# A language-model tower on one core: the front stage's VectorE and ScalarE queues in another order

## The reference

```python
h = L0_tok_W_with_zero_row[x]                        # out-of-range tokens give a row of zeros
# RWKV block on xn = layernorm(h)
xx = shift_by_one_token(xn)
k = (xn*mix_k + xx*(1-mix_k)) @ Wk.T                 # v and r alike
def step((p, q, o), (kt, vt)):
    no = max(o, u + kt)
    y  = (exp(o-no)*p + exp(u+kt-no)*vt) / (exp(o-no)*q + exp(u+kt-no))
    no2 = max(w + o, kt)                             # the running maximum
    return (exp(w+o-no2)*p + exp(kt-no2)*vt, exp(w+o-no2)*q + exp(kt-no2), no2), y
h = h + (sigmoid(r) * y) @ Wo.T
# the next block, on x1 = layernorm(h)
logits = x1 @ w_router.T                             # 4 experts
probs = softmax(logits); gate, idx = top_k(probs over the tokens, 256 of 512)
y = layernorm(x1) * gamma1 + beta1                   # then attention, MLP and the scatter back
```

## Time and profile before

| | |
|---|---|
| median of 3 runs | 2375.97 us |
| the profiled execution: its own time, its span | 2375.98 us, 2374.2 us |
| TensorE busy | 2081.6 us, 88% |
| VectorE busy | 1209.1 us, 51% |
| ScalarE busy | 775.0 us, 33% |
| GpSimd busy | 514.9 us, 22% |
| 100 to 200 us: TensorE, VectorE busy, granted clock | 88.03, 70.64 us, 0.81 |
| 200 to 300 us: the same | 57.61, 76.41 us, 0.59 |
| 300 to 400 us: the same | 31.39, 70.11 us, 0.57 |

### The profile page before, as it was taken

The page is one execution under the profiler, slowest core; times in us unless marked ns, Lnnn a source line. Parts: engine busy times, 40 slices in busy tenths (PEclk is TensorE's granted clock), DMA queues, the critical chain, the costliest instruction groups (busy, mean ns, idle before and its releaser), DMA issues. The chain is left out here.

```text
span 2374.2 us, 29716 instructions
## 1 busy us (share of the span) xinstructions
PE 2081.6 (88%) x10840; PEld 1304.1 (55%) x10848; DVE 1209.1 (51%) x2811; ACT 775.0 (33%) x1330; POOL 514.9 (22%) x718
## 2 busy tenths in 40 slices
PE   4887516899898899986999999879999999999997
PEld 2343313354454454444566666546555878787885
DVE  5776866655755765634766776535711222222221
ACT  2212101445445444544455555312111111111111
POOL 5100113231331322101111111110072222222222
PEclk9977556999999999997999999978999999999999
DMA  3600000000000000000000000020023122222221
GB/s 65 226 11 0 0 1 12 1 1 1 1 1 1 1 1 1 1 1 25 5 6 6 5 6 5 5 90 1 7 87 100 29 60 61 58 55 55 66 33 18
DMA packets 42131, 66.10 MB, mean 28 GB/s; under 512 B 10362, under 2 KB 34206, under 8 KB 39713
## 3 DMA queue, kind: packets, MB, share of 16 engines
q1 hardware_dynamic: 25858, 48.43, 6.3%
q0 software_dynamic: 16128, 15.76, 3.9%
HBM read 35.66 MB, written 30.03 MB: 28 GB/s over the span
## 5 line engine op out<-in xcount | busy, mean ns | idle before, releaser
L1288 ACT ACTIVATE e<-c_ps_s 128x512 f32<-128x512 f32 x384 | 220.6, 598 | 254.0 <-PE c_ps_s L1114 253.2
L928 DVE TENSOR_REDUCE row_max<-c_ps_m 128x1 f32<-128x512 f32 x384 | 255.4, 686 | 63.4 <-PE c_ps_m L1098 57.4
L2585 DVE TENSOR_TENSOR e_f<-e_ps_u,e_gate 128x512 f32<-128x512 f32 x120 | 83.0, 692 | 309.4 <-ACT e_gate L2828 309.4
L2828 ACT ACTIVATE e_gate<-e_ps_g 128x512 f32<-128x512 f32 x120 | 71.6, 597 | 441.2 <-PE e_ps_g L2755 441.2
L2386 POOL DMA_INDIRECT out<-m_o,m_row_of x80 | 125.6, 1570 | 304.8 <-issue 282.8
L1098 PE MATMUL c_ps_m<-c_kT,qT 96*128 96x512 bf16 x384 | 153.5, 400 | 27.2 <-DVE row_max L928 26.2
L1114 PE MATMUL c_ps_s<-qT,c_kT 97*128 97x512 bf16 x384 | 150.1, 393 | 25.5 <-DMA qT<-max_rows 15.1
L2769 PE MATMUL e_ps_o<-m_w,e_f 128*128 128x192 f32 x960 | 166.7, 331 | 1.4 <-DVE e_f L2585 1.4
L2769 PEld LDWEIGHTS e_ps_o<-m_w,e_f 128*128 128x128 f32 x960 | 154.9, 190 | 14.7 <-issue 12.9
L2759 PE MATMUL e_ps_u<-m_xT,m_w 64*128 64x256 f32 x480 | 135.3, 402 | 0.0
L2755 PE MATMUL e_ps_g<-m_xT,m_w 64*128 64x256 f32 x480 | 135.3, 402 | 0.0
(11 more groups left out here) (427 smaller groups left out, 4065.9 us busy)
## 6 DMA issues: line engine op xcount, KB each, us to landing
dealt<-x SPq DMA_DIRECT2D x8, 1290.0 KB, 13.4
m_x<-dealt SPq DMA_DIRECT2D x40, 258.0 KB, 2.7
m_w<-in_w13e SPq DMA_DIRECT2D x8, 1152.0 KB, 5.4
m_w<-in_w2e SPq DMA_DIRECT2D x8, 576.0 KB, 6.6
out<-h SPq DMA_DIRECT2D x8, 384.0 KB, 4.6
c_twice<-conv SPq DMA_DIRECT2D x16, 128.0 KB, 2.3
out<-m_o,m_row_of POOLq DMA_INDIRECT x80, 3.5
e_s<-in_s SPq DMA_DIRECT2D x1, 1152.0 KB, 6.2
```

The lines of the kernel that those rows point to most:

```text
L928: dve.tensor_reduce(row_max[:, n // J, n % J:n % J + 1], ps_m[:, n % 2, :], AX_X, ALU.max)\
L1288: act.activation(e[:, n % LIVE_E, :], ps_s[:, n % 2, :], ACT.Exp, scale=QSCALE).then_inc(e_ready, 1)
```

## The change

On VectorE, exponents 0 moves ahead of the loop, and in the loop exponents p+1 stands behind norm_sums p-1 and ahead of add_rows p. For the last pair, in the same place, stand the statistics and the application of the second block's layernorm (`moe.y`), which were at the end. On ScalarE, the copies of keys p+1 stay together, and exps p+1 stands behind gates p+1 and ahead of routed p-1. On GpSimd, the reciprocal root for `moe.y` moves ahead of the last two of the layernorms in `roots`. TensorE's and SyncE's queues, all sizes and all arithmetic stay.

```diff
--- before.py
+++ after.py
@@ -316,10 +316,11 @@
             kit.apart(pool)
             gather(2)
             gather(3)
-            for n in range(4, 4 * PAIRSEQ, 2):
+            for n in range(4, 4 * PAIRSEQ - 2, 2):
                 roots(n)
             pool.wait_ge(y_var, 1)
             ln_rstd(kit, pool, moe.rstd, moe.var_eps).then_inc(y_rstd, 1)
+            roots(4 * PAIRSEQ - 2)
             pool.wait_ge(moe_in, 7 * 16)
             pool.wait_ge(y_norm, 1)
             y = moe.y[:, :, 0:C]
@@ -453,8 +454,8 @@
 
             norm_rows(0)
             norm_rows(1)
+            exponents(0)
             for p in range(PAIRSEQ):
-                exponents(p)
                 if p + 2 < PAIRSEQ:
                     norm_rows(p + 2)
                 if p > 1:
@@ -462,13 +463,16 @@
                 weighted_means(p)
                 if p > 0:
                     norm_sums(p - 1)
+                if p + 1 < PAIRSEQ:
+                    exponents(p + 1)
+                else:
+                    ln_stats(dve, x1[:, 0:J, :], moe.stats, moe.mv, moe.var_eps, 1e-6).then_inc(y_var, 1)
+                    dve.wait_ge(y_rstd, 1)
+                    ln_apply(dve, moe.y[:, :, 0:C], x1[:, 0:J, :], moe.mv, moe.rstd).then_inc(y_norm, 1)
                 add_rows(p)
             norm_sums(PAIRSEQ - 1)
-            ln_stats(dve, x1[:, 0:J, :], moe.stats, moe.mv, moe.var_eps, 1e-6).then_inc(y_var, 1)
             read_logits(PAIRSEQ - 2)
             dve.memset(ones, 1.0)
-            dve.wait_ge(y_rstd, 1)
-            ln_apply(dve, moe.y[:, :, 0:C], x1[:, 0:J, :], moe.mv, moe.rstd).then_inc(y_norm, 1)
             read_logits(PAIRSEQ - 1)
 
             dve.drain()
@@ -681,18 +685,14 @@
             gates(0)
             for p in range(PAIRSEQ):
                 if p + 1 < PAIRSEQ:
-                    keys(p + 1, 0)
-                    keys(p + 1, 1)
-                    if p > 0:
-                        exps(p)
-                    keys(p + 1, 2)
+                    for i in range(3):
+                        keys(p + 1, i)
                     if p + 2 < PAIRSEQ:
                         turned(p + 2)
                     for i in range(3):
                         values(p + 1, i)
                     gates(p + 1)
-                else:
-                    exps(p)
+                    exps(p + 1)
                 if p > 0:
                     routed(p - 1)
             routed(PAIRSEQ - 1)
```

## The result

| | before | changed | ratio, 95% interval |
|---|---|---|---|
| median of 4 and 4 runs | 2377.18 us | 2360.14 us (2355.1 to 2366.1) | 0.9928 [0.9902, 0.9954] |
| same kernels, second series (11 and 6 runs) | 2380.16 us | 2362.55 us (2351.5 to 2367.3) | 0.9908 [0.9884, 0.9932] |
| same kernels, third series (11 and 6 runs) | 2378.55 us | 2360.20 us (2353.1 to 2366.7) | 0.9918 [0.9900, 0.9935] |

What follows compares the result with a forecast made beforehand. VectorE was taken to carry the front stage's chain, idle 31.7 us for output matmuls and 16.0 us for ScalarE's exponentials. Gains of 7.4, then 23.7, shrinking to 22.3 us in all gave 2375.98 - 22.3 = 2353.7 us, range 2349.5 to 2358.5.

Steps and rivals of the forecast that it cites:

- Pair 0 to 1: Exponents 1 fill VectorE's wait for outputs 0, so `num` of pair 1 starts at 112.9 instead of 120.33 us.
- term of 7.4 us: Gain at the weighted means of pair 1: the 7.5 us of idle time ahead of the additions, less a gap.
- Pair 1 to 2: `num` of pair 2 at 165.2 instead of 188.86 us, 23.7 us gained in all, despite 7.0 us new wait for logits.
- Rival 2: Pair 0's logits find the clock low and take 8.3 instead of 6.0 us: 2356.0 us; chance 0.11.
- Pair 2 to 3: `num` of pair 3 at 219.7 instead of 241.97 us; TensorE idles some 5 us before logits, gain shrinks to 22.3 us.
- The tail: From z of pair 3 to the last read, TensorE carries the chain; the moved `moe.y` work costs nothing there.
- The starting point: The sum started from the profiled execution's 2375.98 us; the median was 2375.97 us.
- The range: 2349.5 to 2358.5 us, from the clock in two groups of logits and the gaps; leaves out two rivals.
- my nine: The forecast's range for the program's time, 2349.5 to 2358.5 us.
- Rival 1: Pair 1's logits find the clock high and take 6.0 us: 2351.4 us; chance 0.16.
- rival 3: TensorE becomes the bound in pair 3, k, v, r staying at half clock: 5.9 us slower, 2381.9 us; chance 0.04.
- rival 4: The gain is given back behind the stage, by the clock or transfers meeting otherwise: 2376 us; chance 0.05.

Runs made afterwards that it cites:

- profile 1: The changed kernel without further edit, first series: last read of logits at 292.90 us, ratio to before 0.9928 [0.9902, 0.9954].
- profile 2: The changed kernel run again without edit, second series: last read of logits at 286.70 us, ratio to before 0.9908 [0.9884, 0.9932].
- profile 3: The changed kernel run a third time without edit, third series: last read of logits at 287.94 us, ratio to before 0.9918 [0.9900, 0.9935].
- second profile of before: The kernel before, run once more unchanged on another chip: last read of logits at 304.90 us, ratio 0.9992 [0.9971, 1.0012].
- two experiments: On the changed kernel, GpSimd's arithmetic made to wait for the last layernorm (ratio 0.9892), or the `moe.y` layernorm and its root put back at the end (0.9906).
- first profile of before: The kernel before, unchanged, as profiled for the forecast: last read of logits at 302.87 us, profiled execution 2375.98 us.
- reads and GpSimd late: On the changed kernel, logits reads behind the weighted means and GpSimd's arithmetic behind the last layernorm, on another chip: last read 268.20 us, ratio 0.9856 [0.9825, 0.9888].

## Why the prediction was right or wrong

The steps from one landmark to the next, in us, forecast and measured (the forecast by its own numbers; a positive miss is late):

| from, to | forecast | profile 1 | profile 2 | profile 3 |
|---|---|---|---|---|
| start of z of pair 0 | 93.5 | 95.2 | 92.9 | 93.1 |
| z of pair 0 to `num` of pair 1 | 19.4 | 22.5 | 22.5 | 19.1 |
| to `num` of pair 2 | 52.3 | 53.9 | 52.2 | 54.4 |
| to `num` of pair 3 | 54.5 | 54.3 | 54.3 | 54.3 |
| to the last read | 60.9 | 67.0 | 64.8 | 67.0 |
| start of the last read, and its miss | 280.6 | 292.9, +12.3 | 286.7, +6.1 | 287.9, +7.3 |

- **Pair 0 to 1.** The term of 7.4 us held where outputs 0 stayed at full clock: `num` of pair 1 at 112.24 in profile 3, 112.9 forecast. "TensorE's outputs 0 end near 103.7 as before" was a level taken from one profile as if it were fixed; in two of three profiles it was not, and 3.1 us of the term went in both. Why it fell there stays open.
- **Pair 1 to 2.** Right in kind: exponentials no longer the releaser, a new wait for the logits, forecast 7.0, measured 9.0, 7.3 and 9.5 us. Rival 2, logits 0 at half clock, came true in two of three profiles at about its price of 2.3 us (7.9 and 8.2 against 6.0). 11% for it was too little. The Trainium skill's rule on transposes (TensorE: Matmul & The Clock Gate, Part 4: PE-mode transpose) had been set aside on one profile; over the 14 the clock does rise in or behind such transposes in some and not in others (in the second profile of before the transposes at 283.9 us ran at 0.67 in the mean). Output matmuls stand ahead of them each time, and no run tries the transposes by themselves, so the rows settle neither the rule nor my reading.
- **Pair 2 to 3.** Right to 0.2 us, by the mechanism and not by luck: outputs 2 at full clock with no gap ahead, copies behind exponentials, logits 1 at half for 8.3 us in all three profiles.
- **The tail.** This is the step that failed: "The edit puts nothing into that", and "If this cover went, at most 3 us would come back". I priced the moved `moe.y` layernorm by its own 3 us of VectorE, and looked at GpSimd's queue only for deadlock. What it releases there, 7.4 us of arithmetic (295.79 us to the end of the sum of the biases in the kernel before), was in no row of mine, and it moved from VectorE's idle time onto VectorE's last layernorm: 5.6 us of stall, 1.3 to 3.6 us of it on the chain, shown by two experiments. The rest of the tail's excess (39.7 against 33.5 us in profile 1) is clock: both groups of logits at half in profiles 1 and 3 cost 4.0 us over the first profile of before (8.2 and 8.2 against 6.4 and 6.0), the transposes ahead of them some 0.9. Before had the second of the groups at half in its second profile, so these levels are in part chance, which the forecast took as fixed too.
- The Trainium skill had that rule (SBUF — State Buffer, SBUF: two separate sides): VectorE, in its fast two-port form, and GpSimd share a pair of ports that one instruction holds whole, while the other engine is blocked. The trace agrees with it: 374 ns alone, up to 2666 ns beside a GpSimd operation of 2.62 us, and the eight VectorE instructions lasted until 281.17 us, as GpSimd's fourth operation did (280.05 + 1.00 = 281.05). The experiments show that GpSimd's arithmetic beside it makes the layernorm slow; that it is by this pair of ports, and that these instructions run in that form, no run here shows. I had not weighed the rule.
- **The starting point.** The sum went from 2375.98 us; the kernel before has medians of 2377 to 2380. With 2378.5 and the same gain the forecast would have been 2356.2.
- **The range** took in two clock levels and no variation of the 2070 us behind the stage. Their spread, 7.4 us between three profiles of one kernel and 15.2 over all, weighs as much as my nine. Rival 1 did not happen (logits 1 took 8.3 us in all three profiles), nor did rival 3 (k, v and r of pair 3 took 29.4 to 30.3 us in the three profiles, 30.4 forecast). Of rival 4 the rows show nothing beyond that spread: 2071.3 us behind the last read in before, 2071.5 to 2078.9 in the changed kernel.

## What to carry to other kernels

When an instruction is moved earlier, follow what it releases on every other engine, and ask what that will run beside; 3 us of cheap work set free 7.4 us of GpSimd arithmetic, which blocked VectorE where it mattered. When a wait is removed, look at the next instruction in the queue that can wait: here two reads of logits that nobody needed yet kept VectorE idle for 18.4 us, and moving them was worth nearly as much again as the change (0.7% on top of 0.8 to 0.9%). And where a loop of waits runs through two queues, reordering one of them may show nothing in the time; try both before giving it up.

## What the runs showed of the hardware that was not expected

- VectorE's normalisation of 128x192 went from 374 to as much as 2666 ns beside GpSimd's tensor arithmetic, and GpSimd's operations kept their pace (y times gamma 1.67 us beside VectorE's work, 1.68 in before, where VectorE waited; from its start to that of the sum of the biases 6.84 and 6.81 us).
- The output matmuls of pair 3, back to back for 15 us behind 20 to 29 us of idle time, stayed at half clock in all 12 profiles without the added matmuls; with 12 other matmuls ahead of them (0.83 in the mean over their 12.7 us) they ran at full for all 8.3 us.
- The same program's time behind the front stage varied by 7.4 us between three executions (2071.5 to 2078.9), code shared by all kernels by 15.2 (2063.7 to 2078.9), and another chip took 2100.2 us there for the kernel before, against 2071.3, and 2118.9 in the profile of "reads and GpSimd late".
